# Which rows of the last product of a two-layer graph network are fetched one by one, with two row numbers in each loaded word

## The reference, cut to what matters

```python
x = _layernorm(x + _L0_gnn_ref(x, src, dst, edge_weight, edge_weight_n2, ...), axis=-1)
x = _layernorm(x + _L1_gnn_ref(x, edge_weight, L1_gnn_weight, L1_gnn_bias, edge_index, 2), axis=-1)

def _L1_gnn_ref(feature, edge_weight, weight, bias, edge_index, mode):   # edge_index = stack([src, dst])
    feature = feature - jnp.mean(feature, axis=0, keepdims=True)
    feature = feature / (jnp.std(feature, axis=0, ddof=1) + 0.0001)
    dst, src = (edge_index[0], edge_index[1])
    support = jax.ops.segment_sum(edge_weight[:, None] * feature[src], dst, num_segments=n)
    return support @ weight + bias
```

## Time and profile before

| | |
|---|---|
| median of 3 runs | 3389.61 us (3389.28 to 3391.82) |
| the profiled execution's own time | 3392.94 us |
| its span, from the first to the last instruction | 3391.1 us |
| the last product, from POOL's first gather to the end | 2342.2 to 3391.1 us |
| POOL's gathers in it | 821, the last at 3368.3 us |
| granted TensorE clock, mean | 0.896 |

### The profile page before, as it was taken

The page is one execution under the profiler, slowest core; times in us unless marked ns, Lnnn a source line. Parts: engine busy times, 40 slices in busy tenths (PEclk is TensorE's granted clock), DMA queues, the critical chain, the costliest instruction groups (busy, mean ns, idle before and its releaser), DMA issues.

```text
span 3391.1 us, 53241 instructions
## 1 busy us (share of the span) xinstructions
PE 2510.9 (74%) x10701; PEld 1834.1 (54%) x10701; DVE 2299.0 (68%) x5460; ACT 1060.2 (31%) x3135; POOL 2511.3 (74%) x2695
## 2 busy tenths in 40 slices
PE   5766766666666666579999999996766666666687
PEld 3555544443444444368888888543444444444565
DVE  8889977777777777657777777786455455555465
ACT  3344333333333333245555555563000000000022
POOL 6777677777777777777777777576777777777775
PEclk8888998889888889789999999998988888777899
DMA  6554344444444444378899899554333333333344
GB/s 167 156 148 126 120 161 155 156 163 157 155 158 154 160 161 154 131 256 282 289 289 291 289 292 293 160 170 142 108 108 107 107 108 108 108 107 106 106 144 118
DMA packets 277824, 565.66 MB, mean 167 GB/s; under 512 B 57265, under 2 KB 124200, under 8 KB 277511
## 3 DMA queue, kind: packets, MB, share of 16 engines
q0 software_dynamic: 119280, 327.58, 30.9%
q1 hardware_dynamic: 148392, 224.77, 21.1%
q10 hardware_dynamic: 9840, 9.98, 0.9%
HBM read 419.19 MB, written 142.88 MB: 166 GB/s over the span
## 4 chain that ended last, share of the span: by engine, by line
POOL 51%; PE 19%; issue 19%; DVE 7%; DMA 2%; ACT 1%; DVEq 1%; SPq 1%; POOLq 0%; ACTq 0%
POOL arena L678 22%; POOL messages L606 21%; PE ps L1208 9%; POOL arena L600 7%; PE ps L1018 6%; PE ps L1241 2%; PE ps L1141 1%; DVE ps L2102 1%; DVE ps L2101 1%; DMA messages<-arena 1%; DMA arena<-messages 1%; ACT arena L787 0%; DVE bn L2083 0%; DVE ps L1662 0%; DVE arena L1863 0%
## 5 line engine op out<-in xcount | busy, mean ns | idle before, releaser
L606 POOL DMA_INDIRECT messages<-arena x832 | 801.4, 963 | 263.6 <-issue 248.4
L600 POOL DMA_INDIRECT arena<-in_x,arena x832 | 789.7, 949 | 271.7 <-issue 247.4
L678 POOL DMA_INDIRECT arena<-x_table,wh x821 | 777.2, 947 | 260.1 <-issue 249.5
L1279 PE MATMUL ps<-arena 128*128 x2048 | 612.8, 457 | 344.6 <-SPq L541 344.3
L1279 PEld LDWEIGHTS ps<-arena 128*128 128x128 f32 x2048 | 449.6, 228 | 514.7 <-issue 443.1
L1018 PE MATMUL ps<-arena 128*128 128x128 f32 x3328 | 447.3, 292 | 134.0 <-ACT arena L724 97.3
L787 ACT ACTIVATE arena<-ps,arena 128x256 f32<-128x256 f32 x832 | 325.8, 474 | 701.3 <-PE ps L1141 468.5
L1018 PEld LDWEIGHTS ps<-arena 128*128 128x128 f32 x3328 | 425.9, 204 | 202.1 <-ACT arena L724 140.4
L1141 PE MATMUL ps<-arena 128*128 128x256 f32 x1664 | 466.1, 431 | 7.7 <-issue 4.1
L2277 DVE TENSOR_TENSOR node_a<-node_a,ps 128x256 f32 x256 | 107.3, 419 | 490.0 <-PE ps L1279 488.4
L1141 PEld LDWEIGHTS ps<-arena 128*128 128x128 f32 x1664 | 361.3, 219 | 77.6 <-issue 23.4
(11 more groups left out here) (293 smaller groups left out, 2999.6 us busy)
## 6 DMA issues: line engine op xcount, KB each, us to landing
arena<-messages SPq DMA_DIRECT2D x464, 260.0 KB
arena<-in_x SPq DMA_DIRECT2D x304, 128.0 KB, 2.8
gate_rows<-arena SPq DMA_DIRECT2D x49, 384.0 KB, 2.4
arena<-gate_rows SPq DMA_DIRECT2D x49, 384.0 KB, 3.0
arena<-in_x,arena POOLq DMA_INDIRECT x832
messages<-arena POOLq DMA_INDIRECT x832, 2.5
arena<-x_table,wh POOLq DMA_INDIRECT x821
arena<-in_x SPq DMA_DIRECT2D x48, 256.0 KB, 2.8
```

The costliest lines, as they stand in the source:

```text
L600: nc.gpsimd.indirect_dma_start(out=big[:, s, j, 0:D], out_offset=None, in_=x, in_offset=bass.IndirectOffsetOnAxis(ap=ids[:, j:j + 1], axis ...
L606: nc.gpsimd.indirect_dma_start(out=messages, out_offset=bass.IndirectOffsetOnAxis(ap=ids[:, j:j + 1], axis=0), in_=big[:, s, j, :], in_off ...
L678: nc.gpsimd.indirect_dma_start(out=last_rows[:, buffer_of(g), j * D:(j + 1) * D], out_offset=None, in_=x1_table, in_offset=bass.IndirectOf ...
L1279: last = nc.tensor.matmul(ps[g % LAST_SUMS][:, 0:D], last_hot[h][:, j, :], last_rows[:, bass.ds(k, 1), j * D:(j + 1) * D].rearrange("p o d ...
```

## The change

- `LATE` names for each group the columns that come singly and how many rows of each: groups 54, 105, 147 and 176 whole, columns 0 and 1 of 196, and 5 rows each of columns 2 and 3 of group 207, the last, whose last 256 places hold ten edges by the edge count (106250 = 415 x 256 + 10). These 20 columns are not gathered by POOL. In the last two columns five rows each are fetched, the other places keep what the buffer held before.
- Two row numbers of 13 bits are packed in one word by DVE (`late_pairs`); one load serves two rows, the one taken out by an AND, the other by a shift.
- ACT issues 208 rows of 54 at the start, eight rows of 105 behind each square, 320 more behind the square root, and then, once `second_freed` is 106, all 512 rows of 176, before the copies of finished tiles. SP issues six rows in a turn instead of four: 304 of 54, 512 of 147, 256 of 196, ten of 207.
- `rows_loaded` semaphores are shared by groups in turn; `late_row` is refilled by SP at groups 55, 106, 148 and 177.

```diff
-LATE = {103: 4, 185: 4, 199: 3}
-LATE_BUFFER = (0, 1, 0)
+LATE = {54: ((0, 1, 2, 3), 128), 105: ((0, 1, 2, 3), 128), 147: ((0, 1, 2, 3), 128), 176: ((0, 1, 2, 3), 128), 196: ((0, 1), 128), 207: ((2, 3), 5)}
+LATE_BUFFER = (0, 1, 0, 1, 0, 1)
...
         def late_rows(engine, g, first, last, batch):
...
-                at = [divmod(r + u, n) for u in range(min(batch, last - r))]
-                ids = [engine.value_load(late_row[0:1, b * GE + p * CPG + j:b * GE + p * CPG + j + 1]).with_bounds(min_val=0, max_val=NT * P - 1)
-                       for p, j in at]
-                for (p, j), v in zip(at, ids):
-                    engine.dma_start(last_rows[p:p + 1, LAST_ROWS + b, j * D:(j + 1) * D],
-                                     x1_table[bass.ds(v, 1), :]).then_inc(S[f"rows_loaded{i}"], 16)
+                at = [divmod(k, len(columns)) for k in range(r, min(r + batch, last), 2)]
+                words = [(p * CPG + columns[n]) // 2 for p, n in at]
+                pairs = [engine.value_load(late_row[0:1, b * GE // 2 + w:b * GE // 2 + w + 1]).with_bounds(
+                    min_val=0, max_val=(NT * P - 1) * (1 + (1 << LOW_BITS))) for w in words]
+                for (p, n), v in zip(at, pairs):
+                    for j, row in ((columns[n], v & ((1 << LOW_BITS) - 1)), (columns[n + 1], v >> LOW_BITS)):
+                        engine.dma_start(last_rows[p:p + 1, LAST_ROWS + b, j * D:(j + 1) * D],
+                                         x1_table[bass.ds(row.with_bounds(min_val=0, max_val=NT * P - 1), 1), :]).then_inc(S[f"rows_loaded{i % RING}"], 16)
...
-            sp.wait_ge(S["back_kept"], 2 * PAIRS)
-            sp.wait_ge(S["back_mm"], 2 * PAIRS)
-            for i, g in enumerate(LATE):
-                sp.dma_start(late_table[i, :, :], back_id[:, g * CPG:(g + 1) * CPG]).then_inc(S["row_kept"], 16)
+            sp.wait_ge(S["sums_done"], 2)
+            sp.dma_start(late_table.rearrange("i p u -> p i u"), late_pairs).then_inc(S["row_kept"], 16)
...
-                if 1 <= g < 101:
-                    at = 112 + (g - 1) * 4
-                    late_rows(nc.sync, 103, at, min(at + 4, 512), 4)
+                if 1 <= g < 52:
+                    at = 208 + (g - 1) * 6
+                    late_rows(nc.sync, 54, at, min(at + 6, 512), 6)
+                if g in (55, 106, 148, 177):
+                    i = (55, 106, 148, 177).index(g) + 2
+                    sp.dma_start(late_row[:, i % 2 * (GE // 2):(i % 2 + 1) * (GE // 2)],
+                                 late_table[i:i + 1, :, :].rearrange("i p u -> i (p u)")).then_inc(S["row_back"], 16)
...
+                if 58 <= g < 144:
+                    at = 0 + (g - 58) * 6
+                    late_rows(nc.sync, 147, at, min(at + 6, 512), 6)
+                if 151 <= g < 194:
...
-            late_rows(nc.scalar, 103, 0, 112, 8)
+            late_rows(nc.scalar, 54, 0, 208, 8)
...
-                    late_rows(nc.scalar, 185, 0 + 4 * (2 * i + s), 0 + 4 * (2 * i + s + 1), 4)
+                    late_rows(nc.scalar, 105, 0 + 8 * (2 * i + s), 0 + 8 * (2 * i + s + 1), 8)
...
-            late_rows(nc.scalar, 185, 96, 512, 8)
-            act.wait_ge(S["row_back"], 48)
-            act.wait_ge(S["second_freed"], 104)
-            late_rows(nc.scalar, 199, 0, 32, 8)
+            late_rows(nc.scalar, 105, 192, 512, 8)
+            act.wait_ge(S["row_back"], 64)
+            act.wait_ge(S["second_freed"], 106)
+            late_rows(nc.scalar, 176, 0, 512, 8)
...
+            for i, g in enumerate(LATE):
+                ids = back_id[:, g * CPG:(g + 1) * CPG].rearrange("p (u j) -> p u j", j=2)
+                link(V.tensor_scalar(late_pairs[:, i, :], ids[:, :, 1], LOW_BITS, None, ALU.logical_shift_left))
+                link(V.tensor_tensor(late_pairs[:, i, :], late_pairs[:, i, :], ids[:, :, 0], ALU.bitwise_or))
+            dve.sem_inc(S["sums_done"], 1)
```

More of the change, by code:

```diff
@@ L110, in gnn_program @@
         weight_row = dram("weight_row", [NT * P])
-        late_table = dram("late_table", [len(LATE), P, CPG], I32)
+        late_table = dram("late_table", [len(LATE), P, CPG // 2], I32)
         node_a = sb("node_a", [P, NTP, D])
@@ L242, in gnn_program @@
         assert PARTS % (4 * RING) == 0 and PARTS <= NG
-        late_row = area(hot_at + 3840, [2 * GE], I32)[0:1, :]
+        late_row = area(hot_at + 3840, [GE], I32)[0:1, :]
+        late_pairs = area(hot_at + 5952, [len(LATE), CPG // 2], I32)
         slot_row = low_tab[0:1, 0:PARTS]
@@ L340, in buffer_of, with late_columns, rows_by @@
             return LAST_ROWS + LATE_BUFFER[list(LATE).index(g)] if g in LATE else (g + 1) % LAST_ROWS
+        def late_columns(g):
+            return LATE[g][0] if g in LATE else ()
         def landed_by(g):
-            return 16 * sum(CPG - LATE.get(k, 0) for k in range(g % LAST_ROWS, g + 1, LAST_ROWS))
+            return 16 * sum(CPG - len(late_columns(k)) for k in range(g % LAST_ROWS, g + 1, LAST_ROWS))
+        def rows_by(g):
+            slot = list(LATE).index(g) % RING
+            return 16 * (2 * XPAIRS // RING + sum(len(c) * n for i, (c, n) in enumerate(LATE.values()) if i % RING == slot and list(LATE)[i] <= g))
         def late_rows(engine, g, first, last, batch):
-            i, n = list(LATE).index(g), LATE[g]
+            i, columns = list(LATE).index(g), late_columns(g)
             b = LATE_BUFFER[i]
             for r in range(first, last, batch):
-                at = [divmod(r + u, n) for u in range(min(batch, last - r))]
-                ids = [engine.value_load(late_row[0:1, b * GE + p * CPG + j:b * GE + p * CPG + j + 1]).with_bounds(min_val=0, max_val=NT * P - 1)
-                       for p, j in at]
-                for (p, j), v in zip(at, ids):
-                    engine.dma_start(last_rows[p:p + 1, LAST_ROWS + b, j * D:(j + 1) * D],
-                                     x1_table[bass.ds(v, 1), :]).then_inc(S[f"rows_loaded{i}"], 16)
+                at = [divmod(k, len(columns)) for k in range(r, min(r + batch, last), 2)]
[6 more added lines that the diff above has]
+                                         x1_table[bass.ds(row.with_bounds(min_val=0, max_val=NT * P - 1), 1), :]).then_inc(S[f"rows_loaded{i % RING}"], 16)
         def scales_of(g):
@@ L522, in _ @@
             gates_load(FULL, 0)
-            sp.wait_ge(S["row_kept"], 16 + 16 * len(LATE))
+            sp.wait_ge(S["row_kept"], 32)
             sp.dma_start(late_row, late_table[0:2, :, :].rearrange("(o i) p j -> o (i p j)", o=1)).then_inc(S["row_back"], 16)
@@ L537, in _ @@
                 if g in LATE:
-                    sp.wait_ge(S[f"rows_loaded{list(LATE).index(g)}"], 16 * (2 * XPAIRS // RING + LATE[g] * P))
-                if LATE.get(g) != CPG:
+                    sp.wait_ge(S[f"rows_loaded{list(LATE).index(g) % RING}"], rows_by(g))
+                if len(late_columns(g)) < CPG:
                     sp.wait_ge(S[f"second_rows{g % LAST_ROWS}"], landed_by(g))
@@ L546, in _ @@
                     sp.sem_inc(S["second_freed"], 1)
-                if g == 104:
-                    sp.dma_start(late_row[:, 0:GE], late_table[2:3, :, :].rearrange("i p j -> i (p j)")).then_inc(S["row_back"], 16)
-                if 1 <= g < 101:
-                    at = 112 + (g - 1) * 4
-                    late_rows(nc.sync, 103, at, min(at + 4, 512), 4)
[L552 to L556, removed]
+                if 1 <= g < 52:
[5 more added lines that the diff above has]
+                                 late_table[i:i + 1, :, :].rearrange("i p u -> i (p u)")).then_inc(S["row_back"], 16)
+                if g in (58, 109, 151, 180):
+                    sp.wait_ge(S["row_back"], 48 + (58, 109, 151, 180).index(g) * 16)
+                if 58 <= g < 144:
+                    at = 0 + (g - 58) * 6
+                    late_rows(nc.sync, 147, at, min(at + 6, 512), 6)
+                if 151 <= g < 194:
+                    at = 0 + (g - 151) * 6
+                    late_rows(nc.sync, 196, at, min(at + 6, 256), 6)
+                if 194 <= g < 196:
+                    at = 0 + (g - 194) * 6
+                    late_rows(nc.sync, 207, at, min(at + 6, 10), 6)
             sp.wait_ge(S["rows_made"], NT + NT - FULL + 2)
@@ L671, in _ @@
                 k = g % LAST_ROWS
-                if LATE.get(g) == CPG:
+                if len(late_columns(g)) == CPG:
                     continue
@@ L676, in _ @@
                     pool.wait_ge(S["second_freed"], g - LAST_ROWS + 1)
-                for j in range(LATE.get(g, 0), CPG):
+                for j in range(CPG):
+                    if j in late_columns(g):
+                        continue
                     nc.gpsimd.indirect_dma_start(
```

## The result

| | before | after |
|---|---|---|
| median (runs) | 3389.45 us (6) | 3403.76 us (6) |
| lowest to highest | 3387.46 to 3391.82 | 3401.64 to 3408.61 |
| the profiled execution's own time | 3392.94 | 3402.79 |
| its span | 3391.1 | 3400.7 |
| from POOL's first gather of the last product to the end | 1048.9 | 1059.4 |

The kernel before has six runs here, three more than when the forecast was made. The ratio is 1.0046 with a 95% interval of 1.0036 to 1.0056: slower by 14.3 us. The forecast was 3395.4 us, with a range of 3384 to 3407. The time lies inside the range, but on its slower side: not within 0.2% of the kernel before, as the likeliest case had it, but some 0.4% above.

The account below looks back on a forecast made before the run. The prediction took POOL's gathers of the last product, 1.251 us each, to bound the kernel. Its terms -11.3 + 19.1 - 2.0 summed to +5.8 us, moving the median from 3389.6 to 3395.4 us, range 3384 to 3407.

Parts of the forecast that it names:

- Columns taken from POOL: Last product: 20 columns come singly instead of 11, nine gathers fewer at 1.251 us each, -11.3 us if POOL never waits.
- A batch of eight rows on ACT: ACT's single rows: with packed row numbers a batch falls from 6.075 to 5.24 us, bounds 4.78 and 6.075.
- ACT's first rows: ACT's 26 batches of group 54 delay the first square by 12 us; PE waits some 8 us, price nothing.
- Group 105: Its rows on ACT land at 2880.6 us; SP stands 12 us, POOL's wait just fits, price nothing.
- A turn of SP with six rows: SP's turn takes 4.6 us, under POOL's 5.0; SP recovers from a delay by only 0.4 us a group.
- Group 176 and the finished tiles: ACT's rows of 176 end at 3231.0 us, delaying the first tile copy; POOL stands before group 179, +19.1 us.
- The last group: End of the last product: PE comes to the last part without a pause; between -2.8 and 0, taken as -2.0 us.
- From the profiled execution to the median: The profiled execution, 3392.94 us, stands 3.3 us above the median, so 3398.7 us becomes a median of 3395.4.
- DVE and the tables: Added DVE packing operations before the first gate step, between nothing and 8 us of work; price nothing, without stock 3 us.
- ACT is in time: Rival, faster: with a batch of 5.05 us or less the copy comes before POOL misses it; 3376 us, chance 0.10.
- SP and ACT get in each other's way: Rival, slower: ACT's issues wait for SP's, a batch 0.24 us longer, 25 us over 104 batches; 3420 us, chance 0.06.
- SP's turn is longer than POOL's group: Rival, slower: turns above 5.005 us cost the excess 19 times from turn 175 to 193; 3401 us at 5.3, chance 0.08.

Follow-up runs that it names:

- run 3: Changed kernel, but the first 56 rows of group 176 are issued by SP in its empty turns 144 to 150; 3380.67 us, ratio 0.9971 to the kernel before.
- runs 7 and 8: Changed kernel: in 7, SP's rows of 147 moved from turns 105-107 to 144-146, 3393.96 us; in 8, 36 rows of 105 moved from ACT to SP, 3394.25 us.
- run 2: Changed kernel, but ACT fetches the 512 rows of group 190 in place of those of 176, which POOL gathers; 3406.89 us.
- runs 9 and 10: The kernel before, unchanged, profiled a second and third time; single times 3386.28 and 3394.59 us.
- run 4: Changed kernel, but POOL gathers group 147 again and SP issues no single rows from turn 58 to 150; 3391.74 us.

## Why the prediction was right and wrong, point by point

**Columns taken from POOL, -11.3 us.** Right. 812 gathers at the old pace; run 3, where nothing else stands in the way, shows the term whole: 1035.2 us from the first gather against 1046.3 for the kernel before as it usually runs, 11.1 us less.

**A batch of eight rows on ACT, 5.24 us.** Measured 5.29. The 0.05 us lie in the addresses (0.46 us a batch, taken as 0.43) and in the loads (1.10 us saved, taken as 1.12). The split of a batch was off without harm: the working took medians, 4.55 us, and called the other 1.52 us gaps, but by the sum of all durations it is 5.06 us and gaps of 1.01, before and after alike, because one load and one issue in each batch are longer than the median. Over 64 batches the 0.05 us make 3.0 us.

**ACT's first rows, nothing.** The first square came at 2477.66 (2478 in the prediction), PE waited 8.15 us for it, and no wait of POOL answers to that.

**Group 105, nothing.** POOL waited only 0.2 us beyond the usual there, as said. SP stood 13.0 us (12). But the wait, and the three turns behind it, set when ACT may begin 176, at 2896.2 us (2895.6 in the prediction, which carries it into the term of 176). The number was right; that this place stood on the path to the end, and was worth 9 to 13 us by itself, the prediction's "nothing" hid, and runs 7 and 8 show.

**A turn of SP with six rows, 4.6 us.** Right for most turns: from the wait at 105 to turn 142 they are 4.6 to 5.2 us apart, 4.7 in the mean. Behind the long wait they take 4.9 in the mean, so SP recovers there by 0.1 us a group and not by 0.4, which run 2 paid for. Of the 0.17 us that a turn is longer there, 0.06 are in its loads and 0.08 in its issues; why is open.

**Group 176 and the finished tiles, +19.1 us.** The mechanism was right in every link: ACT, `final(0)`, turn 174, group 179. This is the term that was mis-sized most: 23.1 us. By links: ACT was through at 3234.6 and not 3231.0 (+3.6, of which 3.0 are the batch); from the copy to POOL's next gather 5.4 us instead of 6.2 (-0.8); and POOL was due at 3217.3 instead of 3218.1, since this execution's stage began 0.9 us earlier (+0.8). The rest, 0.3 us, is what passes between any two gathers, which the profile counts in; without it the wait is 22.8 us. Small waits of POOL for SP add some 0.5 us.

**The last group, -2.0 us.** This step failed. From the last gather to the end it is 20.9 us in the changed kernel, and 19.8 and 20.1 in runs 9 and 10 of the kernel before: about +1, not -2. Against the first profile's 22.8 us it does come to -1.9; but that end came of a last part at half clock which two of three executions don't have, and the prediction took what one execution did for the kernel's habit.

**From the profiled execution to the median, -3.3 us.** The same long end, a second time: of the 3.3 us by which that execution stood above the median, 2.6 were, as far as three profiles tell, in its last product (1048.9 against 1046.3), above all in that end. The sum thus took the end out with the -2.0, and again with the median. Of the 8.4 us between forecast and median, 4.1 lie between the two profiled executions, most of it the term of 176; 3.3 are this step; and 1.0 is what the changed kernel's median stands above its own profiled execution.

**DVE and the tables, nothing.** Right, as far as the spread lets one see: from DVE's first operation on the tables to the first gather 201.7 us, and 199.8 to 201.5 in the three executions of the kernel before.

Against the kernel before as it usually runs, the sum is -11.3 + 23.3 (the wait of 22.8 and the small ones) + 1.0 = +13.0 us, and from the first gather to the end 1059.4 - 1046.3 = 13.1 were measured; the medians say 14.3.

**The rivals.** "ACT is in time" needed 5.05 us a batch and lost to 5.29. The rule beside it, from the Trainium skill, DMA: Bandwidth & Descriptors, "Issuing engines are not separate DMA queues", that the time to initiate a DMA is usually small, does not hold for these rows of 1 KB: a row takes 0.66 us of ACT's time (5.29 / 8), half of the 1.30 us from the issue of the last row of group 105 to its landing, and loading the numbers and issuing them is 13% of the chain that ends last. "SP and ACT get in each other's way" is refuted by run 4: 334.2 against 334.3 us for 512 rows, and 5.25 against 5.27 us for eight where SP was silent in the one. "SP's turn is longer than POOL's group" did not happen in the mean (4.9 against 5.0 us), but came near it behind the long wait.

## What to carry to other kernels

When work moves from the engine that binds to one that seems idle, look up what stands *behind* the new place in that engine's order, and whether the idle time ends before it: here 9 columns off POOL were worth 11 us only where ACT's rows ended before the first tile copy was due (57 batches did, 62 and 64 did not). The remedy was small: 56 of 512 rows moved to empty turns of another queue, and a loss of 0.4% became a gain of 0.3%. The turns have to be empty ones: six rows in each of SP's turns 105 to 107 cost 9 us (run 7). And before a gain is taken from a feature of one profiled execution (a last part at half clock), see whether a second execution has it.

## What was not expected of the hardware

A queue that issues six 1 KB rows in each 5 us didn't slow another queue that issues without a pause: 5.27 us for eight rows of ACT with SP busy, 5.25 with SP silent (2900 to 3050 us, changed kernel and run 4), with a median issue of 225 ns in both. And after a pause of 2 to 3 us PE does a part at full clock in one execution (1.99 us behind 2.89 us of idling) and at half in another (3.77 behind 3.04) of the same kernel, so that this price can't be read from one trace.
